# One 128-row tile for the gate and up rows of the half-filled last chunk

## The chip, the cores and the metric

The kernel runs on one core of a Trainium2 chip. The core has a matrix engine (TensorE, PE in the profile; its weight loads are PEld), a vector engine (VectorE, DVE), a scalar engine (ScalarE, ACT), GpSimd (POOL) and SyncE (SP), which here only issues transfers. The engines run side by side and wait for one another by semaphores. The metric is the device time of one execution in microseconds; lower is better.

## The reference, cut to what matters

Two layers over 32 x 64 = 2048 tokens of 1024 features. Layer 0 (mixing, a gated low-rank layer) and the adapter-dependent linear layer in front of the last feed-forward part are not touched by the change. What the change touches is this part of layer 1, where every weight matrix is replaced by three values (-1, 0, 1) times a scale:

```python
def _bitlinear(x, w):
    scale = jnp.mean(jnp.abs(w))
    q = jnp.round(jnp.clip(w / (scale + EPS), -1.0, 1.0))
    return x @ (q * scale).T
gate = _bitlinear(hidden_states, w_gate)   # [2048, 1024] x [1024, 2752]
up = _bitlinear(hidden_states, w_up)       # the same shape
out = _bitlinear(gate * up, w_down)        # [2048, 2752] x [2752, 1024]
```

The inner size is 2752 = 21.5 x 128: 21 chunks of 128 rows and one of 64.

## The kernel before, in words

All activations lie on chip, transposed, in `act_t` (128 partitions, high and low float16 part, 8 chunks of features, tokens); behind the 2048 tokens it has four dummy blocks of 64 columns. The feed-forward part handles the tokens in four groups of 512 (`NG`).

*Group 0* prepares the weights while it computes. The 22 row chunks (`IC`) are walked in pairs; the chunk with index n has half h = n % 2 and pair p = n // 2, and the two halves of a pair are rows p * 128 and (p + 11) * 128. For each chunk SP loads gate, up and down rows (`load_q`), DVE clips them (`quantize`, L1708), ACT or DVE rounds them (`round_q`), PE turns them (`turn_q`, L910, 8 transposes of each of three kinds), ACT copies them out of PSUM (`store_q`), and PE multiplies (`gate_up`, L938: 16 matmuls of 512 columns for gate and 16 for up). ACT scales the gate product (`scale_gate`), DVE multiplies it with the up product (`product`, L1753). The last chunk has 64 real rows in each of the three tiles and zeros, written by POOL, in the others, but costs PE as much as a full one.

*Groups 1 to 3* use Strassen's scheme in Winograd's form: seven products of half size in place of eight. For this DVE forms sums of weight tiles (`turn_a` for gate and up, `turn_b` for down), and SP stores them to DRAM (`wa_scratch`, `wb_scratch`). For gate and up the two row halves of the 2 x 2 scheme are gate and up, and the columns are the two halves of the 512 tokens. One `unit` on PE (L982) handles a pair of chunks: seven steps (`GATE_STEPS`), each with h = 1 and h = 0 (the two chunks of the pair), 4 feature chunks and 2 parts, so 112 matmuls of 256 columns into four PSUM banks; the bank halves are the chunks of the pair. There are 11 units (`NP`) a group. ACT copies the first product out (`copy_p1`), DVE adds the sums (`unit`, L1764: u2, c22 twice, c12, c21), and multiplies gate by up into `st`, then forms Winograd's sums of the result (`inter_sums`); ACT rounds them to float16 (`high_inter`) and POOL (DVE in group 0) subtracts to get the low part (`low_inter`, L673 and L1729). In the last unit (index 10) h = 1 is the half-filled chunk.

`down(g)` (L1011) multiplies by the down weights with the same scheme: seven steps of 2 x 22 matmuls of 512 columns, weights in two ring buffers that SP loads from `wb_scratch` (`load_products`) one step ahead. Step 0 is split: first the ten pairs 0 to 9 for both token halves (40 matmuls), then pair 10, which waits for `inter_low` of unit 10.

*Order of the work.* Each engine runs its own list, written out by hand, and waits on counted semaphores; nothing reorders it. SP first stores and loads in the order of `load_q`, `store_wa`, `store_wb`, and in front of `down(0)` it waits for all stores of `wb_scratch` (`sp.wait_ge(wb_stored, 16 * NP)`, L575) before it issues the first loads from there (L552).

## Time and profile before

| | us |
|---|---|
| median of 3 runs | 1358.02 (1353.72 to 1361.02) |
| the profiled execution, its own time | 1357.98 |
| its span | 1356.0 |

| engine | busy us | share |
|---|---|---|
| PE matmul | 1321.9 | 97% |
| PE weight load (beside matmuls) | 846.0 | 62% |
| DVE | 720.2 | 53% |
| ACT | 398.2 | 29% |
| POOL | 157.8 | 12% |

A row of the page names a source line, an engine, the operation, the tiles written and read, the count, then busy time and mean duration of one, then the idle time in front and what ended it. "Busy" counts overlapping instructions once, the mean duration of one is longer than its share. The feed-forward part runs from about 499 us to the end: group 0's chunks to 680, `down(0)` to 747, then three times eleven units and a `down`.

### The profile page before, as it was taken

To read this page: it belongs to the slowest core of one execution; us is meant where nothing else is said; L and a number is where in the kernel's file an instruction comes from. 1 tells how busy PE (TensorE), PEld (TensorE's weight loads), DVE (VectorE), ACT (ScalarE), POOL (GpSimd) and SP (SyncE) were. 2 spreads that over 40 slices of the span, in tenths; PEclk is the share of its full clock that TensorE was granted. 3 is DMA by queue.
4 is the path that set the end of the run, shared out by engine and by line. 5 is a ranking of instruction groups with operands and counts; after the bars stand their busy time and mean duration, and the time that the engine had idled before them with its cause. 6 is when DMAs were issued, how large, how long until landed. Compare 5 with 4: busy or idle time off the path is not lost.

```text
span 1356.0 us, 24375 instructions
## 1 busy us (share of the span) xinstructions
PE 1321.9 (97%) x8880; PEld 846.0 (62%) x8881; DVE 720.2 (53%) x1159; ACT 398.2 (29%) x459; POOL 157.8 (12%) x113
## 2 busy tenths in 40 slices
PE   6997999999999999999999999999999999999998
PEld 6873544444444555555544888844888844888843
DVE  6685555211455557888763455581455581455521
ACT  4565334101111258888620121120121120122100
POOL 4100000001011000000000123310222310232210
PEclk9998999999999999999999999999999999999999
DMA  9895899929997759999775543364543355544354
GB/s 311 280 373 202 289 398 407 263 83 260 275 279 197 215 195 323 358 357 360 228 273 184 209 153 129 141 231 171 195 162 145 120 228 186 179 162 162 129 201 148
DMA packets 166275, 310.68 MB, mean 229 GB/s; under 512 B 91042, under 2 KB 123106, under 8 KB 158338
## 3 DMA queue, kind: packets, MB, share of 16 engines
q1 hardware_dynamic: 147506, 242.77, 54.4%
q10 hardware_dynamic: 14352, 44.03, 8.8%
q0 software_dynamic: 4352, 23.01, 4.8%
q8 instruction: 41, 0.67, 0.2%
q14 instruction: 24, 0.20, 0.0%
HBM read 220.78 MB, written 68.03 MB: 213 GB/s over the span
## 4 chain that ended last, share of the span: by engine, by line
PE 79%; DMA 8%; DVE 4%; issue 4%; ACT 3%; POOL 1%; ACTq 1%; DVEq 0%; POOLq 0%; SPq 0%
PE pair L1003 27%; PE pair L1040 18%; PE pair L876 13%; PE pair L932 11%; DMA region_q<-in_L_cond_weight 5%; PE pair L791 5%; PE pair L922 2%; PE pair L690 2%; DMA region_q<-in_L_ffn_weight 2%; DVE region_q L1417 2%; DMA region_w<-in_L_ffn_w_gate 1%; ACT region_q L1072 1%; PE pair L755 1%; PE pair L798 1%; DMA w1s_scratch<-region_q 1%
## 5 line engine op out<-in xcount | busy, mean ns | idle before, releaser
L1003 PE MATMUL pair<-act_t,region_q 128*128 128x256 f16 x3696 | 404.0, 273 | 0.0
L1003 PEld LDWEIGHTS pair<-act_t,region_q 128*128 128x128 f16 x3696 | 361.7, 98 | 42.5
L1040 PE MATMUL pair<-region_q,region_w 128*128 128x512 f16 x1232 | 267.1, 379 | 0.3
L1040 PEld LDWEIGHTS pair<-region_q,region_w 128*128 128x128 f16 x1232 | 120.2, 98 | 146.1 <-POOL region_w L675 1.8
L675 POOL TENSOR_TENSOR region_w<-region_q,region_w 128x1792 f32 (+1 forms) x33 | 118.4, 3587 | 522.0 <-ACT region_w L1319 522.0
L876 PE MATMUL pair<-region_w,act_t 128*128 x816 | 178.9, 379 | 0.0
L791 PE MATMUL pair<-region_w,act_t 128*128 128x512 f16 x768 | 170.6, 379 | 0.0
L932 PE MATMUL pair<-act_t,region_q 128*128 128x512 f16 x704 | 155.5, 379 | 0.0
L876 PEld LDWEIGHTS pair<-region_w,act_t 128*128 x816 | 79.8, 98 | 92.6
L1325 ACT ACTIVATE region_q<-pair 128x512 f32<-128x512 f32 x33 | 19.7, 597 | 398.6 <-PE pair L1003 398.6
L791 PEld LDWEIGHTS pair<-region_w,act_t 128*128 (+1 forms) x768 | 75.1, 98 | 86.7 <-DVE region_q L1656 0.2
L932 PEld LDWEIGHTS pair<-act_t,region_q 128*128 128x128 f16 x704 | 68.0, 98 | 77.9
L1417 DVE SCALAR_TENSOR_TENSOR act_t<-pair,act_t 128x512 f32 (+2 forms) x82 | 61.7, 790 | 95.0 <-ACT act_t L1072 92.7
L1319 ACT ACTIVATE region_w<-region_q 128x1792 f32 (+1 forms) x44 | 74.5, 1694 | 65.2 <-DVE region_q L1751 65.2
L1072 ACT ACTIVATE act_t<-pair 128x512 f32 (+2 forms) x82 | 51.9, 680 | 127.0 <-PE pair L690 99.0
L1825 DVE SCALAR_TENSOR_TENSOR region_q<-pair,out_c,region_q 128x512 f32<-128x512 f32 x32 | 24.0, 750 | 108.7 <-PE pair L1040 108.6
L1778 DVE TENSOR_TENSOR region_q<-pair,region_q 128x512 f32<-128x512 f32 x33 | 22.8, 692 | 90.1 <-PE pair L1003 90.1
L1417 DVE SCALAR_TENSOR_TENSOR region_q<-region_q 128x1024 f16<-128x1024 f32 x41 | 49.5, 1222 | 34.7 <-ACT region_q L1072 34.6
L1282 ACT ACTIVATE region_q<-region_q,inv 128x1024 f32<-128x1024 f32 x55 | 59.6, 1143 | 20.9 <-DVE region_q L1714 20.3
L1298 ACT ACTIVATE region_q<-pair 128x1024 f16<-128x1024 int16 x66 | 63.7, 1022 | 1.8 <-PE pair L922 1.8
L1771 DVE TENSOR_TENSOR region_q<-pair,region_q 128x512 f32<-128x512 f32 x33 | 22.8, 692 | 75.0 <-PE pair L1003 75.0
L1072 ACT ACTIVATE region_q<-region_q 128x1024 f16<-128x1024 f32 x41 | 42.9, 1056 | 48.8 <-DMA region_q<-in_L_cond_weight 38.2
(191 smaller groups left out, 1011.5 us busy)
## 6 DMA issues: line engine op xcount, KB each, us to landing
region_q<-wa_scratch SPq DMA_DIRECT2D x33, 1792.0 KB, 7.4
region_q<-wb_scratch SPq DMA_DIRECT2D x28, 1408.0 KB, 6.1
region_q<-in_L_cond_weight SPq DMA_DIRECT2D x40, 512.0 KB, 9.8
w1s_scratch<-region_q ACTq DMA_DIRECT2D x40, 512.0 KB, 6.9
wa_scratch<-region_q SPq DMA_DIRECT2D x22, 896.0 KB, 6.4
wb_scratch<-region_q SPq DMA_DIRECT2D x11, 896.0 KB, 4.2
region_q<-in_L_ffn_w_gate SPq DMA_DIRECT2D x19, 512.0 KB, 5.7
region_q<-in_L_ffn_w_up SPq DMA_DIRECT2D x19, 512.0 KB, 6.6
```

Source lines behind the costliest of these rows:

```text
L675: pool.tensor_tensor(at(iop[:, 1], u), st[s][:, 0:7], at(iop[:, 0], u), ALU.subtract)\
L690: mm = pe.transpose(dst[:, k * P:(k + 1) * P], src[:, k * P:(k + 1) * P], idn[:, :])
L791: pe.matmul(pair[s][:, h * H:(h + 1) * H], act_t[:, a, k, ds(t * P, P)], w0_t[:, 4 * h:4 * h + 4, b, k, :], start=(k == 0 and a + b == 0), ...
L876: mm = pe.matmul(pair[s][:, h * H:(h + 1) * H], act_t[:, a, c, ds(at, P)], w1_t[:, ds(buf, 1), b, c, h * H:(h + 1) * H].rearrange("p x o - ...
L932: mm = pe.matmul(dst[:, s * H:(s + 1) * H], wa[s][:, first + k // 4, (k % 4) * P:(k % 4 + 1) * P], act_t[:, a, k, 0:GRP], start=(k == 0 an ...
L1003: mm = pe.matmul(bank(s_bank, b)[:, (1 - h) * HALF:(2 - h) * HALF], ring_a[s][:, h, o_a, k], moving[a], start=(opens and h == 1 and k == 0 ...
L1040: mm = pe.matmul(bank(s_bank, b), iop[:, a, p, o_a, tp * P:(tp + 1) * P], ring_b[r][:, p], start=(opens and p == 0 and a == 0), stop=(not ...
L1072: return act.activation(dst, src, ACT.Copy, scale=scale)
L1282: act.activation(tile, tile, ACT.Copy, bias=ROUND, scale=inv[:, kind:kind + 1])\
L1298: act.activation(dst, src, ACT.Copy, bias=-BITS).then_inc(q_out[kind], 1)
L1319: act.activation(at(iop[:, 0], u), st[s][:, 0:7], ACT.Copy).then_inc(inter_high, 1)
L1417: return v.scalar_tensor_tensor(out=dst, in0=src, scalar=scale, in1=hi, op0=ALU.mult, op1=ALU.subtract)
```

## The change

The gate and up rows of the last chunk, 64 each, are put in one 128-row tile: up rows in partitions 0 to 63, gate rows in 64 to 127. It is clipped and rounded once, with scales that differ by partition, turned once and kept in the dummy columns of `act_t` (`w_both`). In each group `last_part` multiplies it with all 512 tokens in the plain way (16 matmuls of 512 columns); the last unit of groups 1 to 3 runs its seven steps for the other chunk alone, with `last_part` between steps 4 and 5, in the bank whose sum has been taken out. ACT scales partitions 64 to 127 into partitions 0 to 63 of `gate_s`, DVE multiplies (`product_last`) after it has set the lower 64 rows of that part of `st` to zero. Of the last chunk nothing is stored in `wa_scratch`, its `turn_a` goes, and the last unit's load is half as long. Counts that semaphores are compared with are adapted (`IC - kind % 2`, `16 * (NP - h)`). The core of the diff:

```diff
         iop = view(region_w, 0, [2, NP, 7, HALF], F16)
+        w_both = act_t[:, 0, :, NTOK:NTOK + P]
...
         mean = sb("mean", [P, 4], F32)
-        clip = sb("clip", [P, 3], F32)
-        nclip = sb("nclip", [P, 3], F32)
-        inv = sb("inv", [P, 3], F32)
+        scales = sb("scales", [P, 3, 4], F32)
+        clip, nclip, inv = [scales[:, i, 0:3] for i in range(3)]
+        clip_both, nclip_both, inv_both = [scales[:, i, 3:4] for i in range(3)]
         inter_c = sb("inter_c", [P, 1], F32)
...
             for kind, src in enumerate((w_gate, w_up)):
+                if last:
+                    eng.wait_ge(q_turned[0], n - 1)
+                    eng.dma_start(wq_gate[h][(LAST, 0)[kind]:(P, LAST)[kind], :], src[rows:rows + LAST, :])\
+                       .then_inc(wq_loaded[h], 16)
+                    continue
                 if not isinstance(p, int) or n >= 2:
                     eng.wait_ge(q_turned[kind], n - 1)
-                eng.dma_start((wq_gate, wq_up)[kind][h][0:cols, :], src[ds(rows, cols), :])\
+                eng.dma_start((wq_gate, wq_up)[kind][h], src[ds(rows, cols), :])\
                    .then_inc(wq_loaded[2 * kind + h], 16)
...
                 if g == 0:
-                    for h in range(2):
-                        store_wa(sp, NP - 1, h, IC - 2 + h)
+                    store_wa(sp, NP - 1, 0, IC - 2)
                 load_products(q0 + 2, STEPS[2][1])
...
                             load_unit(q0 + 7 + 2 * i + s, 2 * i + s, s)
-                    load_unit(q0 + 7 + NP - 1, NP - 1, 0)
+                    sp.wait_ge(step_done, q0 + 7 + NP - 2)
+                    sp.dma_start(ring[0][:, 0:7 * H], wa_dram[NP - 1, :, 0]).then_inc(step_loaded[0], 16)
                     load_products(q0 + 18, STEPS[0][1])
...
-            for kind in range(3):
-                tile = (wq_gate[1], wq_up[1], wq_down[1])[kind]
-                pool.wait_ge(q_turned[kind], IC - 2)
-                wait_if(pool, zeroed, kind)
-                pool.memset(chunked(tile)[:, :, LAST:P] if kind == 2 else tile[LAST:P, :], 0.0).then_inc(zeroed, 1)
+            pool.wait_ge(q_turned[2], IC - 2)
+            pool.memset(chunked(wq_down[1])[:, :, LAST:P], 0.0).then_inc(zeroed, 1)
...
-            def unit(g, i, s):
+            def last_part(dst, g):
+                for k in range(KC):
+                    for a in range(2):
+                        mm = pe.matmul(dst, w_both[:, k], act_t[:, a, k, g * GRP:(g + 1) * GRP],
+                                       start=(k == 0 and a == 0), stop=(k == KC - 1 and a == 1))
+                mm.then_inc(gu_done, 1)
+
+            def unit(g, i, s, alone=False):
                 base = NP * (g - 1) + 2 * i + s
...
                         pe.wait_ge(p1_copied, base + 1)
+                    if j == 5 and alone:
+                        pe.wait_ge(u2_done, base + 1)
+                        last_part(bank(s_bank, 1), g)
                     if j == 5:
...
                         pe.wait_ge(c22_step, 2 * base + 2)
-                    for h in (1, 0):
+                    for h in ((0,) if alone else (1, 0)):
                         for k in range(KC // 2):
...
                                                ring_a[s][:, h, o_a, k], moving[a],
-                                               start=(opens and h == 1 and k == 0 and a == 0),
+                                               start=(opens and (h == 1 or alone) and k == 0 and a == 0),
                                                stop=((not opens or b == 1) and h == 0 and k == KC // 2 - 1
...
                                     pe.wait_ge(inter1_done, NP * g)
+                                    pe.wait_ge(prod_done, IC + g)
                             if j == 0 and part[0] > 0 and tp == 0:
...
                 gate_up(2 * i + 1, 1)
-            turn_q(IC - 1, 1, NP - 1)
+            turn_q(IC - 1, 1, NP - 1, (2, 0))
             gate_up(IC - 2, 0)
-            gate_up(IC - 1, 1)
+            pe.wait_ge(q_out[0], IC)
+            pe.wait_ge(prod_done, IC - 2)
+            last_part(pair[0][:, H:D], 0)
             down(0)
...
                     unit(g, i, 1)
-                unit(g, NP // 2, 0)
+                unit(g, NP // 2, 0, alone=True)
                 down(g)
...
             def round_q(n, h, p):
-                for kind in ((1, 2), (1, 2, 0))[h]:
+                last = isinstance(n, int) and n == IC - 1
+                for kind in (2, 0) if last else ((1, 2), (1, 2, 0))[h]:
                     act.wait_ge(clipped[kind], n + 1)
                     tile = (wq_gate[h], wq_up[h], wq_down[h])[kind]
-                    act.activation(tile, tile, ACT.Copy, bias=ROUND, scale=inv[:, kind:kind + 1])\
+                    scale = inv_both if last and kind == 0 else inv[:, kind:kind + 1]
+                    act.activation(tile, tile, ACT.Copy, bias=ROUND, scale=scale)\
                        .then_inc(rounded[kind] if kind else rounded_odd, 1)
...
+            def store_last():
+                store_q(IC - 1, 1, NP - 1, (2,))
+                act.wait_ge(q_turned[0], IC)
+                act.activation(w_both, q_bank(IC - 1, 0).bitcast(I16).rearrange("p (k c) -> p k c", k=KC),
+                               ACT.Copy, bias=-BITS).then_inc(q_out[0], 1)
+
             def evacuate(m, c, p):
...
                 else:
-                    if not isinstance(m, int) or m < IC - 1:
+                    if isinstance(m, int) and m == IC - 2:
+                        store_last()
+                    elif not isinstance(m, int) or m < IC - 1:
                         store_q(m + 1, 1, p)
...
                 act.activation(gate_s[s], pair[0][:, s * H:(s + 1) * H], ACT.Copy, scale=inter_c[:, 0:1])                   .then_inc(gate_scaled, 1)
+
+            def scale_last(g, dst, src):
+                act.wait_ge(gu_done, IC + g)
+                act.wait_ge(prod_done, IC + g - 2 if g == 0 else IC + g - 1)
+                act.activation(dst, src, ACT.Copy, scale=inter_c[0:LAST, 0:1]).then_inc(gate_scaled, 1)
...
                 act.activation(p1_s, bank((s + g) % 2, 0), ACT.Copy).then_inc(p1_copied, 1)
+
+            def last_p1(g):
+                base = NP * g - 1
+                act.wait_ge(gs_done, 6 * base + 1)
+                act.wait_ge(u2_done, base)
+                act.activation(p1_s[:, HALF:GRP], bank(g % 2, 0)[:, HALF:GRP], ACT.Copy).then_inc(p1_copied, 1)
...
             for m in range(17, IC + 1):
-                scale_gate(m - 1, (m - 1) % 2)
+                if m < IC:
+                    scale_gate(m - 1, (m - 1) % 2)
+                else:
+                    scale_last(0, gate_s[1][0:LAST], pair[0][LAST:P, H:D])
                 if m < IC - 1:
...
                     copy_p1(g, 0, 0)
-                    with act.Fori(0, NP // 2) as i:
+                    with act.Fori(0, NP // 2 - 1) as i:
                         copy_p1(g, 2 * i + 1, 1)
...
                         high_inter(g, 2 * i + 1, 1)
+                    copy_p1(g, NP - 2, 1)
+                    high_inter(g, NP - 3, 0)
+                    last_p1(g)
+                    high_inter(g, NP - 2, 1)
+                    scale_last(g, gate_s[1][0:LAST], bank(g % 2, 1)[LAST:P, :])
                     high_inter(g, NP - 1, 0)
...
             def quantize(n, h, p, last=False):
-                for kind in range(3):
+                if last:
+                    v.wait_ge(stat_step, 8)
+                    v.wait_ge(wq_loaded[h], 16 * p + 32)
+                    v.tensor_scalar(wq_gate[h], wq_gate[h], clip_both, nclip_both, ALU.min, ALU.max)\
+                     .then_inc(clipped[0], 1)
+                    v.wait_ge(zeroed, 1)
+                for kind in (2,) if last else range(3):
                     tile = (wq_gate[h], wq_up[h], wq_down[h])[kind]
-                    if last:
-                        v.wait_ge(zeroed, kind + 1)
                     v.wait_ge(wq_loaded[2 * kind + h], 16 * p + 16)
...
                     inter_sums(s, 3 * p)
+
+            def product_last(g, up, gate, dst):
+                v.memset(st[0][LAST:P, 0:3:2], 0.0).then_inc(stat_step, 1)
+                v.wait_ge(gate_scaled, IC + g)
+                v.tensor_tensor(dst, up, gate, ALU.mult).then_inc(prod_done, 1)
+
+            def last_unit(g):
+                u = NP - 1
+                base = NP * g - 1
+                a, b, c, d = [bank(g % 2, j)[:, HALF:GRP] for j in range(4)]
+                u2, c22, c12, c21, p1 = [t[:, HALF:GRP] for t in (u2_s, c22_s, c12_s, c21_s, p1_s)]
+                steps = 3 * NP + 4 * base
+                v.wait_ge(inter_low, NP * g + u - 1)
+                v.wait_ge(gs_done, 6 * base + 3)
+                v.wait_ge(p1_copied, base + 1)
+                v.tensor_tensor(u2, b, p1, ALU.add).then_inc(u2_done, 1)
+                v.wait_ge(u2_done, base + 1)
+                v.tensor_tensor(c22, c, u2, ALU.add).then_inc(c22_step, 1)
+                v.wait_ge(gs_done, 6 * base + 4)
+                v.wait_ge(c22_step, 2 * base + 1)
+                v.tensor_tensor(c22, d, c22, ALU.add).then_inc(c22_step, 1)
+                product_last(g, bank(g % 2, 1)[0:LAST, :].rearrange("p (a b) -> p a b", a=2),
+                             gate_s[1][0:LAST].rearrange("p (a b) -> p a b", a=2), st[0][0:LAST, 0:3:2])
+                v.wait_ge(gs_done, 6 * base + 6)
+                v.tensor_tensor(c12, c, u2, ALU.add).then_inc(c12_done, 1)
+                v.wait_ge(c12_done, base + 1)
+                v.wait_ge(c22_step, 2 * base + 2)
+                v.scalar_tensor_tensor(out=st[0][:, 7], in0=c12, scalar=inter_c[:, 0:1], in1=c22,
+                                       op0=ALU.mult, op1=ALU.mult).then_inc(st_step, 1)
+                v.wait_ge(step_done, 18 * g - 10 + u)
+                v.tensor_tensor(c21, d, u2, ALU.add).then_inc(c21_done, 1)
+                v.wait_ge(c21_done, base + 1)
+                v.scalar_tensor_tensor(out=st[0][:, 1], in0=a, scalar=inter_c[:, 0:1], in1=c21,
+                                       op0=ALU.mult, op1=ALU.mult).then_inc(inter1_done, 1)
+                v.wait_ge(st_step, steps + 1)
+                v.wait_ge(inter1_done, base + 1)
+                v.wait_ge(stat_step, 9 + g)
+                v.wait_ge(prod_done, IC + g)
+                inter_sums(0, steps + 1)
...
             quantize(3, 1, 1)
+            v.tensor_copy(scales[0:LAST, :, 3], scales[0:LAST, :, 1]).then_inc(stat_step, 1)
+            v.tensor_copy(scales[LAST:P, :, 3], scales[LAST:P, :, 0]).then_inc(stat_step, 1)
             for m in range(1, 4):
...
             for m in range(16, IC + 1):
-                product(m - 1, (m - 1) % 2, (m - 1) // 2, (m - 1) // 2 % 2)
+                if m < IC:
+                    product(m - 1, (m - 1) % 2, (m - 1) // 2, (m - 1) // 2 % 2)
+                else:
+                    product_last(0, pair[0][0:LAST, H:D].rearrange("p (a b) -> p a b", a=2),
+                                 gate_s[1][0:LAST].rearrange("p (a b) -> p a b", a=2), st[0][0:LAST, 0:3:2])
+                    v.wait_ge(stat_step, 9)
+                    v.wait_ge(prod_done, IC)
+                    inter_sums(0, 3 * (NP - 1))
                 if m < IC - 2:
...
                     turn_b(m // 2)
-                if m < IC - 1:
+                if m < IC - 2:
                     turn_a(m + 1, (m + 1) % 2)
...
                     unit(g, i, 1)
-                unit(g, NP // 2, 0)
+                last_unit(g)
                 down(g)
```

## Rows read from the trace of the kernel before

**Rows 1.** The page: busy time, share of the span, instructions of each engine.
```profile
PE 1321.9 (97%) x8880; PEld 846.0 (62%) x8881; DVE 720.2 (53%) x1159; ACT 398.2 (29%) x459; POOL 157.8 (12%) x113
```

**Rows 2.** The page: groups by line; busy us, mean ns, idle us before.
```profile
L1003 PE MATMUL pair<-act_t,region_q 128*128 128x256 f16 x3696 | 404.0, 273 | 0.0
...
L1040 PE MATMUL pair<-region_q,region_w 128*128 128x512 f16 x1232 | 267.1, 379 | 0.3
```

**Rows 3.** Chain that ended last, from 640 us: start, us, what.
```profile
657.08 1.34 PE pair L922 x24
658.42 6.91 PE pair L932 x32
...
680.49 66.65 PE pair L1040 x308
747.14 122.28 PE pair L1003 x1120
```

**Rows 4.** Timeline, end of group 0: start, us, engine, line, [idle before <-releaser].
```profile
665.37 0.69 ACT L1315 ACTIVATE region_w<-pair,inter_c 128x512 f32<-128x512 f32 x1 [0.75 <-PE pair L932]
...
666.09 0.69 DVE L1758 TENSOR_TENSOR region_q<-pair,region_w 128x512 f32<-128x512 f32 x1 [1.40 <-ACT region_w L1315]
...
670.11 0.37 SPq L395 DMA_DIRECT2D wb_scratch<-region_q  x1
...
674.17 1.12 SPq L552 DMA_DIRECT2D region_q<-wb_scratch  x2
...
674.94 2.02 DVE L1731 TENSOR_TENSOR region_w<-region_q,region_w 128x1792 f16<-128x1792 f32 x1
...
680.49 14.57 PEld L1040 LDWEIGHTS pair<-region_q,region_w 128*128 128x128 f16 x69 [0.50 <-DMA region_q<-wb_scratch]
```

**Rows 5.** Timeline of PE in layer 0: its two longest waits.
```profile
25.84 1.09 PE L690 MATMUL pair<-ident,region_q 128*128 128x128 f32 x8 [3.69 <-DMA region_q<-in_L_ffn_weight]
...
128.32 2.74 PE L798 MATMUL pair<-region_q 128*128 128x512 f16 x6 [6.69 <-DVE region_q L1417]
```

**Rows 6.** Stretches behind them: length, busy us of each engine, PEclk (granted clock), DMA.
```profile
26.00:28.00 2.00, 2.00 (x15) 2.00 (x15) 0.00 (x0) 1.02 (x1) 1.17 (x3) 0.73 1.03 373
28.00:32.00 4.00, 4.00 (x27) 3.95 (x26) 1.57 (x2) 1.62 (x3) 1.92 (x4) 0.71 1.05 387
128.32:134.00 5.68, 5.68 (x21) 3.30 (x22) 0.14 (x1) 1.02 (x1) 0.00 (x0) 0.61 0.00 0
```

**Rows 7.** Timeline, end of unit 10 of group 1 and start of `down(1)`.
```profile
872.28 0.42 DVE L1751 TENSOR_TENSOR region_q<-region_q 128x256 f32<-128x256 f32 x1
...
874.79 3.59 POOL L675 TENSOR_TENSOR region_w<-region_q,region_w 128x1792 f32 x1 [8.70 <-ACT region_w L1319]
...
881.36 8.41 PEld L1040 LDWEIGHTS pair<-region_q,region_w 128*128 128x128 f16 x40
881.47 15.77 PE L1040 MATMUL pair<-region_q,region_w 128*128 128x512 f16 x71
881.67 0.69 DVE L1790 TENSOR_TENSOR region_q<-pair,region_q 128x512 f32<-128x512 f32 x1 [0.21 <-PE pair L1003]
882.40 0.75 DVE L1792 SCALAR_TENSOR_TENSOR region_q<-pair,inter_c,region_q 128x512 f32<-128x512 f32 x1
883.25 0.43 DVE L1746 TENSOR_TENSOR region_q<-region_q 128x256 f32<-128x256 f32 x1
...
886.74 3.58 POOL L675 TENSOR_TENSOR region_w<-region_q,region_w 128x1792 f16<-128x1792 f32 x1 [8.36 <-ACT region_w L1319]
886.90 3.70 DVE L1809 TENSOR_TENSOR region_q<-region_q 128x256 f32<-128x256 f32 x1
890.37 6.59 PEld L1040 LDWEIGHTS pair<-region_q,region_w 128*128 128x128 f16 x32 [0.60 <-POOL region_w L675]
```

**Rows 8.** DMA issues, whole run, then 655 to 700 us: KB, median us to landing.
```profile
region_q<-wb_scratch SPq DMA_DIRECT2D x28, 1408.0 KB, 6.1
...
wa_scratch<-region_q SPq DMA_DIRECT2D x3, 896.0 KB, 11.7
```

More of the change, by code:

```diff
@@ L576, in _ @@
             for kind in range(3):
-                sp.wait_ge(q_turned[kind], IC)
+                sp.wait_ge(q_turned[kind], IC - kind % 2)
             for s in range(2):
@@ L594, in _ @@
                         for h in range(2):
-                            sp.wait_ge(wa_stored[h], 16 * NP)
+                            sp.wait_ge(wa_stored[h], 16 * (NP - h))
                     load_unit(q0 + 7, 0, 0)
@@ L1023, in down @@
                                     for kind in range(3):
-                                        pe.wait_ge(q_out[kind], IC)
+                                        pe.wait_ge(q_out[kind], IC - kind % 2)
                             if j == 0 and part[0] == 0 and tp == 1:
@@ L1334, in down @@
                         for h in range(2):
-                            act.wait_ge(wa_stored[h], 16 * NP)
+                            act.wait_ge(wa_stored[h], 16 * (NP - h))
                     if g > 0:
@@ L1831, in down @@
                         for h in range(2):
-                            v.wait_ge(wa_stored[h], 16 * NP)
+                            v.wait_ge(wa_stored[h], 16 * (NP - h))
                     else:
@@ L1879, in _ @@
             v.wait_ge(stat_step, 1)
-            v.tensor_scalar(clip[:, :], mean[:, 0:3], Q_EPS, None, ALU.add).then_inc(stat_step, 1)
+            v.tensor_scalar(clip, mean[:, 0:3], Q_EPS, None, ALU.add).then_inc(stat_step, 1)
             v.tensor_scalar(out_c[:, :], mean[:, 2:3], 1.0 / INTER_SCALE, None, ALU.mult).then_inc(stat_step, 1)
@@ L1885, in _ @@
             v.wait_ge(stat_step, 4)
-            v.tensor_scalar(nclip[:, :], clip[:, :], -1.0, None, ALU.mult).then_inc(stat_step, 1)
-            v.reciprocal(inv[:, :], clip[:, :]).then_inc(stat_step, 1)
+            v.tensor_scalar(nclip, clip, -1.0, None, ALU.mult).then_inc(stat_step, 1)
+            v.reciprocal(inv, clip).then_inc(stat_step, 1)
             v.wait_ge(stat_step, 6)
```

## The prediction

> **What bounds the kernel now.** The share of busy time comes first: TensorE (PE) is busy 97% of the span [rows 1]. That is an average over stages, so I went on to the groups of instructions by line, which give PE's price per instruction: 404.0 us / 3696 = 109.3 ns for a 256-column matmul of a gate and up unit, 267.1 / 1232 = 216.8 ns for a 512-column one of the down projection [rows 2]. Each row's own "mean ns" is longer because neighbours overlap. The chain that ended last shows that PE itself is the path in this half of the kernel: 24 transposes 1.34 us, a 32-matmul gate and up chunk of group 0 6.91 us, down(0) 66.65 us, and 1120 unit matmuls (ten units) 122.28 us, so 12.23 us a unit [rows 3]. Work taken off PE is therefore worth its whole time, except where PE would then arrive early at something else. The timeline at the two junctions into `down` tells that.
>
> **Group 0.** PE loses 16 of 64 matmuls of `gate_up(IC - 1, 1)` (half of 32, at 6.91 / 32 = 0.216 us) = 3.45 us, and 8 of 24 transposes of `turn_q(IC - 1, ...)`, 8 x 1.34 / 24 = 0.45 us: 3.90 us of work [rows 3]. What it meets then is the load of the first down weights. SP issued it at 674.17, 4.06 us after the last store of `wb_scratch` (670.11), for whose landing it waits; PE had already waited 0.50 us when its first weight load for `down(0)` went at 680.49 [rows 4]. Does the change move that load? The store waits for `turn_b(10)`, which follows on DVE `product` of chunk 19 (666.09) and its sums; that product waits for ACT's scaling at 665.37, and this for a PE chunk in front of everything the change touches [rows 4]. The shorter quantize, round and copies in front fill time in which ACT and DVE waited for PE, and the four `turn_a` operations that go lay behind `turn_b`. The store of the last half of `wa_scratch` that goes is issued behind the load. So the load lands at about 680.4 as before, and the 3.90 us come back as a wait: gain 0 (bounds: 0.5 us lost if the landing shifts, 0.5 gained if it is one store lighter). The other condition, `low_inter` of unit 9, starts at 674.94 [rows 4] once ACT has scaled chunk 20; with 8 transposes fewer that is 0.45 us earlier and ends before 677. The chain behind `last_part` (scale, product, sums, high, low, some 8 us) ends about 3.5 us earlier too, under 20 of 40 matmuls of step 0.
>
> **What the new wait does to the clock.** PE now stands still for about 3.9 - 0.2 = 3.7 us ahead of `down(0)`. The trace has two waits of that kind: one of 3.69 us [rows 5], after which the granted clock was 0.73 over 26 to 28 us and 0.71 over 28 to 32 us (full speed is 1, the lower level 0.5) [rows 6], that is 0.27 x 2 + 0.29 x 4 = 1.7 us lost; and one of 6.69 us [rows 5], after which it was 0.61 over 5.68 us [rows 6], 2.2 us lost. PE was not idle as long anywhere else, and outside these the clock stood at full speed. The matmuls behind the first wait were small f32 ones, here they will be dense 512-column f16 ones, so it is not certain. I take a fall, and 1.9 us for it, the middle of the rows; bounds 0 and 2.5. The Trainium skill (TensorE: Matmul & The Clock Gate, Why this matters for your kernels) says the same against this change: idle gaps of some microseconds between bursts of matmuls send the clock back to half. By that rule the sum has the 1.9 us in it, without it not; the trace agrees in both of its long gaps.
>
> **Groups 1 to 3, each.** The last unit runs one half of its columns: 56 of 112 matmuls go, 56 x 109.2 ns = 6.11 us [rows 3]. `last_part` adds 16 matmuls of 128x512 x 216 ns = 3.46 us [rows 2, 3]: 2.65 us less. That its weights come from the same tensor as the moving operand is in no row; bounds 216 ns a matmul, and 98 ns more if weight loads were no longer covered (4.7 us over the three groups), which I hold unlikely, as weight loads of 98 ns run beside every matmul now. Waits inside the unit: with t = 0 at the unit's start (869.24 in group 1, 12.23 before 881.47) `last_part` is reached at 40 x 0.109 = 4.37, that is 873.61. It needs `u2_done`; DVE is busy with unit 9's sums until 872.28 + 0.42 = 872.70 [rows 7], then adds for 0.4, so 0.5 us to spare. `p1_copied` comes some 2 us before step 4. `down` is reached at 881.47 - 2.65 = 878.8; it needs `low_inter` of unit 9, which POOL ended at 874.79 + 3.59 = 878.38 [rows 7]: 0.4 us to spare where there were 3.1. No new wait, but little room. The `wb_scratch` load for step 0 lands 6.1 us after its issue at about 869.4 (median of 28 loads) [rows 8], 3.3 us before it is needed. The weights of the last unit are half a load now, never late.
>
> **The chain at the junction.** Between the first 40 matmuls of `down` and the last 4 of step 0 PE waits for unit 10 to pass DVE, ACT and POOL. Now: unit end to 881.67, then 0.73, 0.85, sums from 883.25, POOL 886.74 to 890.32, PE's weight load at 890.37, 9.01 us after 881.36; the 40 matmuls take 40 x 216.5 = 8.66, so about 0.35 us are lost each time (the row shows 0.60 because weight loads run ahead) [rows 7]. After: `c21` and the last multiply are half as wide. The trace has only 512-column forms of these (0.69 and 0.75 us) and 256-column SBUF additions (0.42 to 0.43) [rows 7]; I take 0.43 and 0.48. But DVE now has `product_last` in front. `gu_done` comes two half steps (16 x 0.109 = 1.75) before the unit's end; ACT starts 0.21 later, DVE 0.72 after that (665.37 to 666.09) [rows 4], so the product runs from -0.82 to -0.10 relative to the unit's end, then `c12` 0.52, its multiply 0.46, `c21` 0.46, the last multiply 0.58: sums start at +1.92, now at 883.25 - 881.47 = +1.78. So the wait grows by 0.14 us. Bounds: 0.35 less (chain shorter, DVE free) and 1.27 more (narrow operations as long as wide ones). Behind the waiting matmul on PE is all of `down`, so it counts in full.
>
> POOL's subtraction also holds DVE: a 0.42 us addition took 3.70 us beside it [rows 7]. The Trainium skill (SBUF — State Buffer, Two separate sides) has this as an exclusive lock for operations with two SBUF inputs. By it `product_last` (one input in PSUM) goes free, and the multiply of `c12` at about 879.2 would meet the lock only if POOL ran past 878.4; no row has a narrower margin, and the sum is unchanged unless it is missed.
>
> **The sum**, against the profiled execution (span 1356.0 us, its own time 1357.98, the median 1358.02, so one base): 3 x (-2.65 + 0.14) = -7.5; group 0 0; clock +1.9. 1358.0 - 7.5 + 1.9 = 1352.4 us. Memsets on POOL and DVE (64 rows), the three-way `scales` tile and its two copies lie beside PE: they run where DVE and POOL waited for ACT or PE; price 0, at most the 0.3 us of one short DVE operation per group.
>
> **The rivals.**
> - *The clock holds.* The matmuls behind the wait are denser than in either row. Then 1350.5. For it: no row has a 3.7 us gap between dense f16 bursts. Against it: both long gaps ended at 0.5.
> - *The load is not the gate.* If the first down weights came with PE's own progress, group 0 would give its 3.9 us, no wait and no clock fall: 1358 - 7.5 - 3.9 = 1346.6. Against it: the 4.06 us from store to load and PE's 0.50 us wait for DMA.
> - *The DVE chain is not narrowed.* 3 x 1.13 = 3.4 us more: 1355.8. For it: short operations have a fixed part (0.42 for 256 columns against 0.69 for 512); against it, that fixed part is only a fifth.
> - *Slower: step 0 of `down` gets a late load in every group.* The wb load must land by 878.8, 9.4 us after issue, and stores to `wa_scratch` took 11.7 us to land in a crowd [rows 8]. It decides from 9.4 us; from 12 us on each group loses more than 2.65 and the kernel is slower than before. At 15 us: 3 x 5.6 = 16.8 us of waits, 1352.4 + 16.8 = 1369. Against it: nothing but this load runs there, and it took 6.1 us.
>
> **Chances.** Forecast (gain of 7.5, clock falls) 0.48; clock holds 0.30; chain not narrowed 0.10; load not the gate 0.06; slower 0.04, rest 0.02. This kernel's measurement tells 0.5%, 6.8 us, from no change, so "faster" starts at 1351.2: the clock-holds case (most of it), the gate case and the low part of the forecast case give faster 0.42; same 0.53; slower 0.05. Eight in ten: 1348.5 to 1356.
>
> **What would show it.** The first `down` matmul still about 14 us after the end of the transposes of chunk 21, with a wait of about 3.7 us for `wb_scratch` in front; granted clock 0.5 for some 4 us behind it, or not; units of 10 x 12.23 us and a last one of 9.6; the wait for POOL 0.4 to 0.7 us in three places; 3696 - 168 = 3528 unit matmuls. I am wrong if down(0) starts before 678, if waits appear inside the last unit, or if the new matmuls take much more than 216 ns.

## The result and the profile after

The changed kernel takes 1350.6 us (median of 7 runs, 1349.27 to 1353.3), the kernel before 1357.08 us in the same comparison (7 runs, 1353.72 to 1361.02): ratio 0.9952, 95% interval 0.9937 to 0.9967. The forecast was 1352.4, range 1348.5 to 1356. The prediction counted from 1358.0, the median of three runs; measured from 1357.08 its gain of 5.6 us would have given 1351.5, so 0.9 of the 1.8 us between 1352.4 and 1350.6 is the base. The total does not tell the forecast from its first rival: with the clock held the prediction had 1350.5. What tells them apart is the trace. The profiled execution took 1350.37, its span is 1348.7 where it was 1356.0.

The page of the changed kernel: busy time by engine, then groups by line (busy us, mean ns of one, idle us before).

```profile
PE 1312.9 (97%) x8736; PEld 833.1 (62%) x8737; DVE 715.3 (53%) x1163; ACT 398.1 (30%) x460; POOL 155.8 (12%) x111
...
L1016 PE MATMUL pair<-act_t,region_q 128*128 128x256 f16 x3528 | 386.1, 273 | 0.0
...
L1054 PE MATMUL pair<-region_q,region_w 128*128 128x512 f16 x1232 | 268.7, 381 | 4.1 <-DMA region_q<-wb_scratch 4.1
```

The share of PE is the same 97% [rows 1] and says nothing. The rows by line say two things: the unit matmuls are 3528, at 386.1 / 3528 = 109.4 ns (109.3 before), and the down matmuls, which nobody touched, have a wait of 4.1 us for a DMA and 1.6 us more busy time than in [rows 2]. Both stand in one place of the chain of the changed kernel (start, us, what):

```profile
669.19 4.05 DMA wb_scratch<-region_q
...
673.26 6.49 DMA region_q<-wb_scratch
...
679.80 68.34 PE pair L1054 x308
748.14 126.63 PE pair L1016 x1160
874.77 3.45 PE pair L988 x16
878.22 1.75 PE pair L1016 x16
879.97 66.63 PE pair L1054 x308
946.60 126.63 PE pair L1016 x1160
```

Before, PE led straight into `down(0)` [rows 3]. Now a store and a load stand in front of it (669.19 to 679.75), and `down(0)` takes 68.34 us where it took 66.65 and where `down(1)` takes 66.63. PE's own timeline shows the wait, and the table by stretch of the changed kernel (length, busy us of PE, PEld, DVE, ACT, POOL, PEclk, DMA share, GB/s) what it did to the clock:

```profile
672.05 3.62 PE L988 MATMUL pair<-act_t 128*128 128x512 f16 x16
679.80 20.42 PE L1054 MATMUL pair<-region_q,region_w 128*128 128x512 f16 x86 [4.13 <-DMA region_q<-wb_scratch]
```

```profile
679.80:682.00 2.20, 2.20 (x6) 0.87 (x7) 1.34 (x1) 0.82 (x1) 0.00 (x0) 0.54 0.95 225
682.00:684.00 2.00, 2.00 (x7) 0.75 (x6) 0.68 (x1) 0.00 (x0) 0.00 (x0) 0.65 0.92 352
684.00:686.00 2.00, 2.00 (x11) 0.88 (x9) 0.00 (x0) 0.00 (x0) 0.00 (x0) 1.00 0.59 247
```

The last `gate_up` and `last_part` end at 675.67, the next matmul goes at 679.80. Behind that the granted clock is 0.54 and 0.65 (0.46 x 2.2 + 0.35 x 2 = 1.7 us lost), only 6 and 7 matmuls of 512 columns go where a stretch of 2 us has 11 at full clock.

**Where the 7.3 us of the span are.** Up to `turn_q` of chunk 21 (665.16 before, 664.25 after) 0.9 us, in a part that the change doesn't touch: this point lies between 660.8 and 667.0 in the profiles of all kernels here, by waits and by falls of the clock in layer 0. I therefore count from it. From it to the first down matmul 15.33 us before, 15.55 after: +0.2. `down(0)` +1.7. Each later group, start to start, 201.25 us before (747.14 to 948.39) and 198.46 after (748.14 to 946.60): 3 x -2.79 = -8.4. From `turn_q` to the end of the span that is 690.8 before and 684.45 after, -6.4.

The junction into `down(1)` of the changed kernel, to be held against [rows 7]:

```profile
878.26 0.69 ACT L1346 ACTIVATE region_w<-pair,inter_c 64x512 f32<-64x512 f32 x1 [2.83 <-PE pair L988]
...
878.98 0.68 DVE L1816 TENSOR_TENSOR region_q<-pair,region_w 64x512 f32<-64x512 f32 x1 [3.31 <-ACT region_w L1346]
879.59 0.41 DVE L1836 TENSOR_TENSOR region_q<-pair,region_q 128x256 f32<-128x256 f32 x1
...
879.81 10.46 PE L1054 MATMUL pair<-region_q,region_w 128*128 128x512 f16 x47
880.03 0.48 DVE L1839 SCALAR_TENSOR_TENSOR region_q<-region_q,inter_c 128x256 f32<-128x256 f32 x1
880.43 0.42 DVE L1842 TENSOR_TENSOR region_q<-pair,region_q 128x256 f32<-128x256 f32 x1
880.88 0.48 DVE L1844 SCALAR_TENSOR_TENSOR region_q<-pair,inter_c,region_q 128x256 f32<-128x256 f32 x1
881.46 0.43 DVE L1795 TENSOR_TENSOR region_q<-region_q 128x256 f32<-128x256 f32 x1
...
884.95 3.58 POOL L678 TENSOR_TENSOR region_w<-region_q,region_w 128x1792 f16<-128x1792 f32 x1 [5.67 <-ACT region_w L1350]
```

The product (L1816) runs from 0.83 to 0.15 us ahead of `down`'s first matmul (879.81), and the sums (L1795) start 1.65 us after it.

### The profile page after: what moved, and what is told of

The parts are those of the page before. It is cut to its first block, busy times and chain, and to the rows that moved or that the text cites. A ratio compares the mean times of both kernels' runs of the same rounds, so it can differ in the third digit from the quotient of the medians.

```text
span 1348.7 us, 24068 instructions
## 1 busy us (share of the span) xinstructions
PE 1312.9 (97%) x8736; PEld 833.1 (62%) x8737; DVE 715.3 (53%) x1163; ACT 398.1 (30%) x460; POOL 155.8 (12%) x111
## 4 chain that ended last, share of the span: by engine, by line
PE 83%; DMA 7%; DVE 5%; ACT 2%; issue 1%; ACTq 1%; DVEq 0%; SPq 0%
PE pair L1016 29%; PE pair L1054 20%; PE pair L879 13%; PE pair L935 10%; DMA region_q<-in_L_cond_weight 6%; PE pair L794 5%; PE pair L693 2%; PE pair L925 2%; DVE region_q L1462 2%; PE pair L758 1%; ACT region_q L1088 1%; PE pair L801 1%; PE pair L988 1%; ACT act_t L1088 1%; DMA region_q<-wb_scratch 0%
## 5 line engine op out<-in xcount | busy, mean ns | idle before, releaser
L1016 PE MATMUL pair<-act_t,region_q 128*128 128x256 f16 x3528 | 386.1, 273 | 0.0
L1016 PEld LDWEIGHTS pair<-act_t,region_q 128*128 128x128 f16 x3528 | 345.0, 98 | 41.5
L935 PE MATMUL pair<-act_t,region_q 128*128 128x512 f16 x672 | 148.6, 379 | 0.0
L935 PEld LDWEIGHTS pair<-act_t,region_q 128*128 128x128 f16 x672 | 64.8, 98 | 74.2
L1300 ACT ACTIVATE region_q<-region_q,scales 128x1024 f32<-128x1024 f32 x54 | 58.6, 1142 | 20.2 <-DVE region_q L1763 19.5
L1866 DVE TENSOR_TENSOR region_q<-pair,region_q 128x512 f32<-128x512 f32 x30 | 20.7, 691 | 81.7 <-PE pair L1016 81.7
L1859 DVE TENSOR_TENSOR region_q<-pair,region_q 128x512 f32<-128x512 f32 x30 | 20.7, 691 | 69.1 <-PE pair L1016 69.1
```

What stands on the lines that cost most here:

```text
L935: mm = pe.matmul(dst[:, s * H:(s + 1) * H], wa[s][:, first + k // 4, (k % 4) * P:(k % 4 + 1) * P], act_t[:, a, k, 0:GRP], start=(k == 0 an ...
L1016: mm = pe.matmul(bank(s_bank, b)[:, (1 - h) * HALF:(2 - h) * HALF], ring_a[s][:, h, o_a, k], moving[a], start=(opens and (h == 1 or alone) ...
L1300: act.activation(tile, tile, ACT.Copy, bias=ROUND, scale=scale)\
```

## The experiments

Times from `turn_q` of the last chunk, all from profiles; the wait is PE's for `wb_scratch` ahead of `down(0)`; `down(0)` is counted from its first matmul; the clock is the mean granted clock over the timed runs.

| kernel | to first down matmul | wait | down(0) | `turn_q` to end | median us | clock |
|---|---|---|---|---|---|---|
| before | 15.33 | (0.50, weight load) | 66.65 | 690.8 | 1358.2 | 0.9955 |
| changed | 15.55 | 4.13 | 68.34 | 684.45 | 1350.6 | 0.9936 |
| changed, again | 15.51 | 4.10 | 69.04 | 685.1 | 1351.3 | 0.9926 |
| last_part twice | 15.62 | 0.75 | 66.65 | 682.8 | 1346.65 | 0.9962 |
| half of it more | 15.36 | 2.23 | 66.65 | 682.6 | 1350.3 | 0.9942 |
| early load | 12.71 | 1.29 | 66.65 | 679.9 | 1345.4 | 0.9957 |
| early load, reordered | 11.45 | none | 66.64 | 678.8 | 1344.4 | 0.9964 |
| cut in the kernel before | 15.30 | 3.43 | 68.34 | 692.5 | 1360.3 | 0.9939 |
| last_part at the end | 15.39 | 3.97 | 68.34 | 685.8 | 1351.6 | 0.9946 |
| early load, reordered, in before | 15.15 | none | 66.64 | 690.7 | 1358.5 | 0.9945 |

(The kernel before: 1358.2 us and 0.9955 in the 11 runs beside "changed, again", "last_part twice" and the two early loads; 1358.3 and 0.9952 in the 24 runs beside the other four; 1357.08 beside "changed".)

**The changed kernel again.** No edit.

> The changed kernel once more, as the base for the kernels run beside it. About 1350.6 us; PE waits some 4.1 us for the first down weights, the down stage of group 0 takes 68.3 us where it took 66.65 before the change (1.7 us of it half clock).

As expected, with a deeper fall: 2.4 us lost.

```profile
682.50:684.00 1.50, 1.50 (x4) 0.57 (x5) 0.62 (x1) 0.85 (x1) 0.00 (x0) 0.50 1.13 255
684.00:686.00 2.00, 2.00 (x6) 0.72 (x5) 1.40 (x1) 0.00 (x0) 0.00 (x0) 0.50 0.75 251
686.00:688.00 2.00, 2.00 (x8) 0.76 (x7) 0.00 (x0) 0.00 (x0) 0.00 (x0) 0.66 0.94 393
```

A third profile of it:

> A third look at the changed kernel: a wait of 4.1 us for the down weights and down(0) at 68.3 to 69.1 us, if a wait of that length lowers the clock every time; 66.65 us if only in some executions.

A wait of 3.95 us and 69.45 us for `down(0)`, 2.8 us lost, a little beyond the 68.3 to 69.1 us expected. So the clock fell in three of three profiles of this kernel, at 1.7, 2.4 and 2.8 us. With the two kernels below that also wait over 3 us at this place (3.43 and 3.97) it is five of five.

**More work for PE in group 0.** `last_part` of group 0 goes through its 16 matmuls twice.

```diff
-                for k in range(KC):
+                for k in ((*range(KC), *range(KC)) if again else range(KC)):
```

> Group 0 alone: last_part runs twice over (16 matmuls more, 3.45 us of work without use). Theory (PE only waits there for the down weights, and that wait lets the clock fall): the wait shrinks from 4.1 to about 0.7 us, the first down matmul stays at the same distance from the chunks before it, the clock holds, down(0) takes 66.7 us, and the kernel is 1.7 us faster than the changed kernel although PE does more. Rival A (the wait hides the work but the slow clock has another cause, such as the switch to other matmuls): no difference. Rival B (the load is not the gate): 3.45 us slower.

The theory holds at each point in the trace. PE's timeline in this kernel:

```profile
671.91 7.07 PE L988 MATMUL pair<-act_t 128*128 128x512 f16 x32
679.73 20.46 PE L1054 MATMUL pair<-region_q,region_w 128*128 128x512 f16 x94 [0.75 <-DMA region_q<-wb_scratch]
```

The first down matmul is as far from `turn_q` as in the changed kernel (15.62 and 15.55), `down(0)` is back at 66.65 us, and the rest of the kernel is 1.7 us shorter than with 3.45 us less work: ratio to before 0.9921 (0.9908 to 0.9935) against 0.9955 (0.9941 to 0.9969) of the changed kernel run beside it. The medians of the two differ by 4.7 us, more than the 2.3 us of their traces from `turn_q` on (685.1 - 682.8). The traces show where more can come from: layer 0, which neither edit touches, lost 8.5 us to a lowered clock in the profile of "changed, again", 5.1 in this one and 3.4 in that of "changed". Whether the other 2.4 us of the medians are longer falls behind the wait or such falls in layer 0 is not shown.

**Half of that.**

```diff
+            for k in range(KC // 2):
+                for a in range(2):
+                    pe.matmul(pair[0][:, H:D], w_both[:, k], act_t[:, a, k, 0:GRP], ...)
             last_part(pair[0][:, H:D], 0)
```

> As the run with last_part twice over in group 0, but with only 8 matmuls more (1.73 us). PE's wait for the down weights becomes about 2.4 us; the first down matmul does not move. Where the clock falls by the length of the wait, this is the point between 0.7 us (held, down(0) 66.65 us) and 4.1 us (fell twice, 68.3 and 69.0). Theory (a wait of this length is too short): held, 66.65 us, as fast as with 16 more. Rival (any wait of more than a matmul or two for the load is enough): it falls, 68 to 69 us.

In the trace the clock holds after a wait of 2.23 us.

```profile
676.48 23.70 PE L1054 MATMUL pair<-region_q,region_w 128*128 128x512 f16 x109 [2.23 <-DMA region_q<-wb_scratch]
```

Its median, though, is 3.6 us above that of the doubled version, with a lower mean clock. Two more profiles of it:

> The kernel with 8 matmuls more in group 0 once more, one look at another time: its first profile had a wait of 2.2 us and a clock that held. If a wait of 2.2 us is too short to lower the clock, down(0) takes 66.65 us again. If it falls in some executions (which would explain that its median, 1350.3 us, stands above what its trace says), 68 to 69 us.

> A third look at the same kernel; as the second: 66.65 us if the wait of 2.2 us is too short, 68 to 69 us if the clock falls in some executions.

Waits of 2.11 and 2.27 us, 66.65 us both times, 1346.5 and 1346.2 us. So after waits of 2.1 to 2.3 us at this place the clock held in three of three profiles. Four of its six timed runs took 1350 to 1351 us at a granted clock of 0.993 to 0.994. Where it fell in those runs no trace shows, so that stays open. Layer 0 alone could make up such a difference, since there waits of the same length end either way. These are "changed, again", then the early, reordered load, at the same matmul of layer 0, each with a stretch behind it (PEclk is the third number from the right), and last a wait of "last_part at the end" and the stretch behind it:

```profile
31.37 3.16 PE L758 MATMUL pair<-region_w,region_q 128*128 128x128 f32 x16 [2.04 <-DVE act_t L1462]
...
34.00:36.00 2.00, 2.00 (x16) 1.71 (x16) 1.37 (x3) 1.61 (x4) 1.38 (x3) 0.50 1.07 379
...
30.88 2.02 PE L764 MATMUL pair<-region_w,region_q 128*128 128x128 f32 x16 [2.04 <-DVE act_t L1473]
...
34.00:36.00 2.00, 2.00 (x17) 1.82 (x16) 2.00 (x4) 1.44 (x4) 1.38 (x3) 1.00 1.04 368
...
505.41 2.33 PE L925 MATMUL pair<-ident,region_q 128*128 128x128 f16 x24 [1.95 <-DVE cnt L1999]
...
506.00:507.00 1.00, 1.00 (x12) 1.00 (x10) 1.00 (x3) 0.17 (x1) 0.00 (x0) 0.50 0.85 352
```

Eight of the profiles wait 2.04 or 2.05 us at that matmul: behind it three lost 5.1 us ("changed, again", the third profile of "changed", the early load), two lost 1.7, in a fall that began only some 5 us after the wait, and three nothing. At the other place, early in group 0, the wait of 1.95 us was followed by a loss of 1.7 us, the waits of 1.26 to 1.77 us of the other twelve profiles by none. So "2.2 us is too short" is shown for the junction into `down(0)`, where 512-column f16 matmuls stand on both sides, and not for any wait of this length.

**The load early.** The first down weights in three pieces; PE's order as it was.

```diff
+            for kind in range(3):
+                sp.wait_ge(q_turned[kind], IC - 1)
+            sp.wait_ge(wb_stored, 16 * (NP - 1))
+            sp.dma_start(ring_b[1][:, 2:NP - 1], wb_dram[STEPS[0][1], :, 2:NP - 1]).then_inc(early_loaded, 16)
             store_wb(sp, NP - 1)
...
-                    load_products(0, STEPS[0][1])
+                    sp.dma_start(ring_b[1][:, 0:2], wb_dram[STEPS[0][1], :, 0:2]).then_inc(early_loaded, 16)
+                    sp.dma_start(ring_b[1][:, NP - 1:NP], wb_dram[STEPS[0][1], :, NP - 1:NP]).then_inc(step_loaded[1], 16)
...
+                                    pe.wait_ge(early_loaded, 32)
```

> The first down weights are loaded in three pieces: pairs 2 to 9 as soon as their place is free (about 15 us earlier), pairs 0, 1 and 10 behind the last store as now; PE's order is unchanged. Theory (store, then load of 1408 KB, is the gate): the late pieces are 3/11 of the bytes and land some 3 to 3.5 us earlier, the wait is 0.6 to 1.2 us, the clock holds: 3 + 1.7 = about 4.7 us faster than the changed kernel (1346). Rival (the 6.3 us from issue to landing are mostly fixed, not bytes): the pieces land 0 to 1 us earlier, and it is 0 to 1 us faster, with the clock still falling.

The chain of this kernel at the junction:

```profile
669.72 4.61 DMA wb_scratch<-region_q
...
674.73 2.71 DMA region_q<-wb_scratch
...
677.49 66.65 PE pair L1061 x308
```

The late load takes 2.71 us in place of 6.49, `down` starts 2.8 us earlier, the clock holds: 684.45 - 679.9 = 4.5 us in the trace, and 1345.37 us, ratio 0.9915 (0.9899 to 0.993). That is slightly short of what was expected: the start moved by 2.8 us and not 3 to 3.5, and the wait is 1.29 us and not 0.6 to 1.2, since the store in front took 4.61 us where it took 4.05, and the load's start behind it slipped by another 0.4. So most of the 6.5 us was bytes, and the load was the gate.

**The load early, and the order turned.** In addition PE takes pairs 2 to 9, then 0 and 1, then 10 in step 0 of group 0.

```diff
+                for part in (((*range(2, NP - 1), 0, 1), range(NP - 1, NP)) if q == 0 ...
+                                if q == 0 and p == 0 and tp == 0:
+                                    pe.wait_ge(early_loaded, 32)
```

> As the early load, and PE takes pairs 2 to 9 first in step 0, then 0 and 1, then 10. Theory: no wait at the junction (at most 0.3 us for low_inter of unit 9), the whole 3.9 us of removed work and the 1.7 us of clock come out: 5.3 to 5.6 us faster than the changed kernel, 1345. Rival (something else is late next there, such as low_inter of unit 9 or the late pieces ahead of pairs 0 and 1): a wait of 1 us or more moves to it and less than 4.5 us is gained.

PE's timeline in this kernel shows no wait:

```profile
661.66 7.07 PE L941 MATMUL pair<-act_t,region_q 128*128 128x512 f16 x32
668.57 3.62 PE L994 MATMUL pair<-act_t 128*128 128x512 f16 x16
672.22 28.00 PE L1065 MATMUL pair<-region_q,region_w 128*128 128x512 f16 x129
```

`down` starts 11.45 us after `turn_q` in place of 15.55: 4.1 us, and 1.7 of clock. Less 0.2 us that the first eleven units of the last group took longer in this trace (126.81 us in place of 126.63) it is 5.6 in all (684.45 - 678.8), as worked out. 1344.37 us, ratio 0.9904 (0.989 to 0.9918): the lowest median of all versions. Its lead over the early load alone is 1.1 us in the traces (679.9 - 678.8); the two intervals overlap.

**The cut alone, in the kernel before.** `gate_up(IC - 1, 1)` computes only its gate half in group 0; this kernel leaves out the up product of the last chunk, which the result needs.

```diff
-            gate_up(IC - 1, 1)
+            gate_part(IC - 1, 1, pair[0], 2).then_inc(gu_done, 1)
```

> The kernel before, with one edit: in group 0 the 16 matmuls of the up half of the last chunk are left out (its up product isn't computed). PE has 3.45 us less to do. Theory: nothing of it is gained, PE waits some 3.7 us for the down weights, and the clock falls: down(0) 68.3 to 69.0 us in place of 66.65, so the kernel is 1.5 to 2.5 us slower than before with less work. Rival (clock holds): the same time as before. Rival (load is no gate): 3.45 us faster.

```profile
664.60 10.52 PE L932 MATMUL pair<-act_t,region_q 128*128 128x512 f16 x48
678.56 21.72 PE L1040 MATMUL pair<-region_q,region_w 128*128 128x512 f16 x92 [3.43 <-DMA region_q<-wb_scratch]
```

With 3.45 us less work it is slower: 68.34 us for `down(0)`, `turn_q` to end 692.5 against 690.8, 1360.32 us against 1358.3, ratio 1.0015 (1.0001 to 1.0028). The interval only just leaves out no difference; what carries the point is the trace, where PE waits 3.43 us, the first down matmul stays where it was (15.30 us behind `turn_q`, 15.33 before) and `down(0)` is 1.7 us longer.

**last_part behind the last step**, in groups 1 to 3 (DVE's `product_last` moved with it).

```diff
-                    if j == 5 and alone:
-                        pe.wait_ge(u2_done, base + 1)
-                        last_part(bank(s_bank, 1), g)
...
+                if alone:
+                    pe.wait_ge(u2_done, base + 1)
+                    last_part(bank(s_bank, 1), g)
```

> The changed kernel with last_part behind the last step of the unit in groups 1 to 3 (and DVE's product_last behind its other work). Theory (chain by engine timings): the product ends 1.6 us after the last matmul, as the sums start there now (1.65 us), so the wait at the junction stays as it is; DVE's additions have about 0.4 us less than nothing to spare at step 6, so a wait of 0 to 0.5 us per group: 0 to 1.5 us slower. Rival (the place between steps 4 and 5 covers much DVE time): 1 us or more per group slower, 3 us or more.

A group takes 198.92 us in place of 198.46 (747.49 to 946.41), so 0.5 us each. The total is inside the 0 to 1.5 us expected. The way there is not: the wait stands at the junction, which was expected to stay as it was. The medians (1351.6, against 1350.6 and 1351.3) are too near to show it; the traces do. Its timeline, end of unit 10:

```profile
875.05 3.58 POOL L678 TENSOR_TENSOR region_w<-region_q,region_w 128x1792 f32 x1 [8.69 <-ACT region_w L1350]
875.49 3.42 DVE L1837 SCALAR_TENSOR_TENSOR region_q<-region_q,inter_c 128x256 f32<-128x256 f32 x1
...
879.16 8.80 PE L1054 MATMUL pair<-region_q,region_w 128*128 128x512 f16 x40
...
879.93 0.48 DVE L1814 MEMSET region_q<- 64x512 f32 x1 [0.16 <-issue]
880.45 0.68 DVE L1816 TENSOR_TENSOR region_q<-pair,region_w 64x512 f32<-64x512 f32 x1
881.26 0.42 DVE L1795 TENSOR_TENSOR region_q<-region_q 128x256 f32<-128x256 f32 x1
...
888.39 1.90 PE L1054 MATMUL pair<-region_q,region_w 128*128 128x512 f16 x8 [0.44 <-POOL region_w L678]
```

The multiply of `c12` now falls beside POOL's subtraction of unit 9 and takes 3.42 us where it takes 0.48 in the changed kernel. Everything of DVE behind it is late, the sums start 881.26 - 879.16 = 2.1 us after the first down matmul in place of 1.65, and PE waits 0.44 us for POOL again. The sentence of the Trainium skill that the prediction weighed (SBUF — State Buffer, SBUF: two separate sides: an exclusive lock between VectorE, for operations with two SBUF inputs, and GpSimd) is borne out here: the operation with both inputs in `region_q` was held, the addition with one in PSUM that had started ahead of it (875.03) was not.

**The early load without the change.** The two edits of the early, reordered load in the kernel before.

> The early load in three pieces and the order 2 to 9, 0, 1, 10, put in the kernel before, without the change. Theory (the load is late there by 0.5 us at most): 0 to 0.5 us faster than before, where the same edit gave 5.6 us on top of the change. Rival (the early load helps by itself): 2 us or more faster than before.

1358.51 us against 1358.3, ratio 0.9999 (0.9988 to 1.001); in the trace it is 0.1 us faster (690.8 and 690.7). The load costs next to nothing there, since PE comes only when it has landed.

## Why the prediction was right, step by step

*Group 0 gives nothing, since the first down weights gate it.* Right: +0.2 us instead of 0, with the load at 6.49 us instead of 6.3 (6.19 to 6.57 over the profiles in which PE waits for the whole load, so 0.2 is within what varies). The wait was 4.13 us and not 3.7: all of the 3.9 us of work and the 0.2 of the load; for the 0.2 us that the prediction took off there was no row. Shown by the doubled `last_part` (start unmoved), the early loads (start 2.8 and 4.1 us earlier) and the cut in the kernel before.

*The wait lowers the clock, 1.9 us.* Right, and 1.7, 2.4 and 2.8 us in three profiles; the rival in which it holds fell with the first. The prediction had 48% on this, and the doubt about denser matmuls behind the wait was unfounded. But its evidence was thinner than it said. It wrote that PE was not idle as long anywhere else and that both long gaps ended at 0.5. The trace of before has a third gap, of 5.23 us at the start of the program, with a granted clock of 1.00 behind it:

```profile
5.23 0.26 PE L706 MATMUL pair<-region_w 32*1 32x32 f32 x2 [5.23 <-DVE region_w L1431]
...
4.00:8.00 4.00, 2.40 (x16) 2.04 (x16) 3.07 (x19) 0.00 (x0) 1.09 (x2) 1.00 0.98 378
```

No work of PE stands in front of that gap in the trace, so it is no clear case against, but it had to be named. The size was in part luck: 1.9 us was the middle of two rows, and the same kernel lost 1.7, 2.4 and 2.8. The Trainium skill's rule that idle gaps of some microseconds between bursts of matmuls send the clock back (TensorE: Matmul & The Clock Gate, Why this matters for your kernels) agrees with the falls after 3.4 to 4.1 us and with none after 0.75 to 2.3 us at this place. At the two other places the traces differ from a rule by length alone: the clock fell behind waits of 1.95 to 2.05 us in six profiles and held behind waits of 2.04 us in three. There the measurement decides.

*Groups 1 to 3, 2.65 us each.* Right: eleven units and `last_part` take 126.63 + 3.45 + 1.75 = 131.83 us, before 881.47 - 746.98 = 134.49, so 2.66. Weights and moving operand from one tensor cost nothing extra: 3.45 / 16 = 216 ns.

*The wait at the junction grows by 0.14 us.* Wrong in sign, and the reason that the sum came out 0.8 us too small (3 x -2.79 in place of 3 x -2.51). The step that failed is the length of DVE's chain: from product to `c12` it is 0.61 us, not 0.72, from `c12` to its multiply 0.44, not 0.52, from there to `c21` 0.40, not 0.46, so the sums start at +1.65, not +1.92, and ahead of the +1.78 of before. The wait before was mis-sized as well, which touches only the bound: I took 9.01 - 8.66 = 0.35 us from the weight loads [rows 7], but `down(1)` took 66.76 us from its first matmul (881.47 to 948.23) against 66.63 without a wait, so only 0.13 were lost. All of the 0.13 us went. The wait for POOL of 0.4 to 0.7 us that was to be seen in three places is there only in the row of the weight loads (0.47 us), not in that of the matmuls.

*Narrow operations cost 0.43 and 0.48.* Right: 0.41 to 0.42 and 0.48. The rival "not narrowed" is gone. So is "slower by a late load in every group": PE has no wait there.

*Small operations at price 0.* The 64-row memset takes 0.48 us (the bound was 0.3) and lies where DVE waits for ACT.

In sum, from `turn_q` on: forecast -7.5 + 1.9 = -5.6; the three profiles -6.4, -5.7 and -5.5 (690.8 less 684.45, 685.1 and 1351.9 - 666.55 = 685.35). In the first of them 0.8 us too little gain at the junctions stands against 0.2 us too much clock and 0.2 us in group 0 that was not forecast.

## What to carry to other kernels

Before PE work is taken out, look at what PE would meet next: here 3.9 us of it ran into a load whose start hung on another chain, and the wait then lowered the clock and cost 1.7 to 2.8 us more. A cut can then be worth less than nothing, and useless matmuls in its place can pay. Find what the transfer itself waits for and split it: the part whose bytes are long there can be loaded early, and an order of work that begins with that part turned a loss of 5.6 us into the full gain.

## What was not expected of the hardware

- One and the same wait (3.95 to 4.13 us) cost 1.7, 2.4 and 2.8 us of clock in three executions. In layer 0 waits of 2.04 to 2.05 us at one matmul cost 5.1 us, 1.7 us or nothing, while waits of 2.1 to 2.3 us ahead of `down(0)` cost nothing in three profiles.
- Moving a DVE operation by 4 us, off its place behind POOL's instruction, made it seven times as long (0.48 to 3.42 us), on engines that were both far from busy.
- The weight-load row of a wait (0.60 us) overstated PE's loss (0.13 us) fourfold, since weight loads run ahead of the matmuls.
